# A gated recurrence inside a four-part kernel: a PSUM bank for each gate, the order i, g, o, and the cell in PSUM

## The chip, the cores and the metric

The kernel runs on one core of a Trainium2 chip. The metric is the time on the device in microseconds (us). Three runs of the kernel before gave 1126.01, 1126.28 and 1126.47 us, a median of 1126.28 us.

## The reference

The input `x` has 32 sequences of 256 positions with 128 features; `adj` has a 256x256 matrix for each sequence. Four blocks follow one another, each with a layer normalisation in front and a residual addition behind: a graph convolution on the first 25 positions, a recurrence over all 256 positions, a graph convolution on all of them, and a mixture of eight experts of which two are used for each token. The change touches only the recurrence:

```python
def step(carry, xs):
    h, c = carry
    xi_t, xf_t, xg_t, xo_t = xs
    i_t = jax.nn.sigmoid(xi_t + h @ V_i)
    f_t = jax.nn.sigmoid(xf_t + h @ V_f)
    g_t = jnp.tanh(xg_t + h @ V_c)
    o_t = jax.nn.sigmoid(xo_t + h @ V_o)
    c_new = h * c + i_t * g_t
    h_new = o_t * jnp.tanh(c_new)
    return ((h_new, c_new), h_new)
```

The gate f is computed and never used: the new cell takes `h * c`, not `f * c`. So three gates count, i, g and o. Each of the 256 steps needs the h of the step before it.

## The kernel before

Everything is written out by hand: five instruction queues (TensorE, VectorE, ScalarE, GpSimd, SyncE), each worked off in its order, with semaphores between them. No planner is at work.

The first 90 us or so hold the loads, the preparation of the weights and the small graph convolution. Then come the 256 steps of the recurrence, in 32 groups (`G`) of eight steps (`s` = 0 to 7). Then come the last two blocks, 16 passes over two sequences each.

The state lies transposed: 128 hidden features on the partitions and the 32 sequences along the free dimension. h is kept as two fp16 parts, `h1` (scaled by 1024 and rounded) and `h2` (what is left), and each V matrix as three bf16 parts. One step is this ring:

- TensorE (line 594, the function `gate`) adds `V @ h` onto PSUM, where the input part `U @ x` and the bias already lie. It waits for `h1`, does three products for each of i, o and g, waits for `h2`, and does two products each for i and o, raises `io_ps`, then two for g, and raises `g_ps`. These are 15 matmuls of 32 columns.
- ScalarE takes the sigmoid of i and o together (line 827, 64 elements in each partition, into `S`), then the tanh of g (line 829, into `GC`).
- VectorE forms the new cell with one scan (line 1111). `S` and `GC` interleave two values for each sequence, so that the scan gives first g and then i * g + h * c. The result `CC` lies in SBUF.
- ScalarE takes the tanh of the cell (line 831, `tanh_c`).
- VectorE forms h from o and `tanh_c` twice: as fp16 `h1` (line 1113), which TensorE waits for, and as fp32 `hs` (line 1114). Then come `h2` (line 1116) and the product h * c for the next step (line 1117, into `GC`).

Each engine has other work in its queue behind its part of the step, chosen by `s`. On VectorE this is `fill`: the normalised input of the next group at s = 0 (`xn`, line 1056), the output rows `x2s` at s = 1 (line 1045, which reads PSUM), statistics at s = 2 and 3, at s = 4 a piece of the adjacency matrix and the normalised output `ys` (line 1040), at s = 5 the scaled adjacency matrix `adjs` (line 1090), statistics at s = 6 and 7. On TensorE: transposes of the last group's h at s = 0 (line 611), of `xn` at s = 1 (line 562), the input products `U @ x` of the next group at s = 3, 4 and 5 (`x_gate`, line 568, fp32, 256 columns, two instructions for each), four transposes of `adjs` at s = 6 (line 626), the biases of the next group at s = 7 (line 573). On ScalarE: row sums of the adjacency matrix at s = 0 and 1 (lines 835 and 840), a copy of the transposed input out of PSUM at s = 2 (line 813), and at s = 6 and 7 a small copy (line 844) and a scaled copy of the transposed adjacency matrix into `adjT` (line 845).

The eight PSUM banks in the recurrence: i and o share one bank and g has one, both doubled for alternate groups (banks 0 to 3); bank 4 holds the transposes of `xn`, bank 5 those of h, bank 6 those of `adjs`; bank 7 is free.

Of the kernel before, what the change touches and what calls it, by code (L numbers as in the profile page):

```python
# [21 lines left out]
ALU = mybir.AluOpType  # L22
# [3 lines left out]
P = 128  # L26
# [47 lines left out]
def build(nc, io):  # L74
    x_in, adj_in, out = io["x"], io["adj"], io["out"]

    with ExitStack() as ctx:
# [45 lines left out]
        with ExitStack() as rec:  # L123
# [8 lines left out]
            CC = sb("CC", [P, B, 2], where=rec)  # L132
# [66 lines left out]
        def pair(name, shape, dt=F32):  # L199
# [38 lines left out]
        (io_ps, g_ps, gates_ready, cell_ready, tanh_ready, h1_ready, h32_ready, h2_ready, hc_ready,  # L238
# [3 lines left out]
            "io_ps", "g_ps", "gates_ready", "cell_ready", "tanh_ready", "h1_ready", "h32_ready", "h2_ready", "hc_ready",  # L242
# [21 lines left out]
        g_bank, io_bank = [PB[0], PB[1]], [PB[2], PB[3]]  # L264
        io_v = [p[:].rearrange("p (q n) -> p q n", q=2) for p in io_bank]
# [11 lines left out]
        def iterations(eng, body):  # L277

            body(0, 0, 0)
            with eng.Fori(0, NB2 // 2 - 1) as it:  # L280
                body(it * 2 + 1, 1, it)
                body(it * 2 + 2, 0, it + 1)
            body(NB2 - 1, 1, NB2 // 2 - 1)

# [4 lines left out]
        def _(sp):  # L289
# [53 lines left out]
            sp.wait_ge(adjT_ready, 2 * NGRP)  # L343
# [15 lines left out]
        def _(pool):  # L359
# [23 lines left out]
            tp.memset(S[:], 0.0).then_inc(gates_ready, 1)  # L383
            tp.memset(GC[:], 0.0).then_inc(hc_ready, 1)
# [102 lines left out]
        def _(pe):  # L487
# [77 lines left out]
            def x_gate(k, q):  # L565

                o = g_bank[k][:, 0:STEPS * B] if q == 2 else io_v[k][:, q, :]
                mm(o, us[:, q, :], xbuf[:], start=(q != 1), stop=False, skip_group_check=True)  # L568

            def biases(k):  # L570
                for q in range(3):
                    o = g_bank[k][:, 0:STEPS * B] if q == 2 else io_v[k][:, q, :]
                    mm(o, brow[:, q, :], ones3[:], start=False, stop=False, skip_group_check=True)
# [5 lines left out]
            pe.wait_ge(xbuf_ready, 1)  # L579
            for q in (0, 1, 2):  # L580
                x_gate(0, q)
            biases(0)
            pe.wait_ge(state_ready, 3)

            with pe.Fori(0, NGRP // 4) as it:
                for q4 in range(4):
                    G, k = it * 4 + q4, q4 % 2
                    for s in range(STEPS):
                        t = it * (4 * STEPS) + (q4 * STEPS + s)
                        cols = slice(s * B, (s + 1) * B)  # L590

                        def gate(q, p, h):
                            o = g_bank[k][:, cols] if q == 2 else io_v[k][:, q, cols]
                            return mm(o, vp[p][:, q, :], h[:], start=False, stop=True, skip_group_check=True)  # L594

                        pe.wait_ge(h1_ready, t + 1)
                        for q in (0, 1, 2):
                            for p in range(3):
                                gate(q, p, h1)
                        pe.wait_ge(h2_ready, t + 1)  # L600
                        for q in (0, 1):
                            for p in range(2):
                                m = gate(q, p, h2)
                        m.then_inc(io_ps, 1)
                        for p in range(2):
                            m = gate(2, p, h2)
                        m.then_inc(g_ps, 1)

                        if s == 0:
                            for i in range(2):  # L610
                                m = tr(PB[5][:, i * P:(i + 1) * P], hs[1 - k][:, i * P:(i + 1) * P], ident)
                            m.then_inc(hT_ps, 1)
                        if s == 1:
                            pe.wait_ge(xn_ready, G + 2)
                            x_transpose()
                        if s in (3, 4, 5):
                            if s == 3:
                                pe.wait_ge(xbuf_ready, G + 2)
                            x_gate(1 - k, s - 3)
                        if s == 7:  # L620
                            biases(1 - k)
                        if s == 6:
                            pe.wait_ge(a_scaled, G + 1)
                            for c in range(2):
                                for n in range(2):
                                    m = tr(PB[6][:, c * T + n * P:c * T + (n + 1) * P], adjs[:, n, c * P:(c + 1) * P], ident)  # L626
                            m.then_inc(aT_ps, 1)
            pe.wait_ge(h2_ready, T + 1)
            for i in range(2):
                m = tr(PB[5][:, i * P:(i + 1) * P], hs[1][:, i * P:(i + 1) * P], ident)  # L630
# [77 lines left out]
            pe.wait_ge(adjT_ready, 2 * NGRP)  # L708
# [49 lines left out]
        def _(act):  # L758
# [61 lines left out]
            with act.Fori(0, NGRP // 4) as it:  # L820
                for q4 in range(4):
                    G, k = it * 4 + q4, q4 % 2
                    for s in range(STEPS):
                        t = it * (4 * STEPS) + (q4 * STEPS + s)
                        cols = slice(s * B, (s + 1) * B)
                        act.wait_ge(io_ps, t + 1)
                        av(S[:, :, :, 1], io_v[k][:, :, cols], ACT.Sigmoid, scale=1 / SC)  # L827
                        act.wait_ge(g_ps, t + 1)
                        av(GC[:, :, 0], g_bank[k][:, cols], ACT.Tanh, scale=1 / SC).then_inc(gates_ready, 1)  # L829
                        act.wait_ge(cell_ready, t + 1)  # L830
                        av(tanh_c[:], CC[:, :, 1], ACT.Tanh).then_inc(tanh_ready, 1)  # L831

                        if s == 0:
                            act.wait_ge(adj_loaded[k], it * 32 + (q4 // 2 * 16 + 16))
                            av(junk[:], adjn[k][:, 0, :], ACT.Copy, accum_out=deg[:, 0:1])
                        if s == 2:
                            act.wait_ge(xT_ps, G + 2)
                            x_evacuate().then_inc(xbuf_ready, 1)
                        if s == 1:
                            av(junk[:], adjn[k][:, 1, :], ACT.Copy, accum_out=deg[:, 1:2]).then_inc(deg_ready, 1)  # L840
                        if s in (6, 7):
                            c = s - 6
                            act.wait_ge(aT_ps, G + 1)
                            av(junk[:, 0:1], ident[:, 0:1], ACT.Copy)
                            av(adjT[:, bass.ds(G, 1), c, :].rearrange("p o n -> p (o n)"), PB[6][:, c * T:(c + 1) * T], ACT.Copy,
                               scale=dinv[:, c:c + 1]).then_inc(adjT_ready, 1)
# [64 lines left out]
        def _(dve):  # L911
# [131 lines left out]
            def h_scaled_add(G, i):  # L1043

                return v.scalar_tensor_tensor(out=x2s[:, i, :], in0=PB[5][:, i * P:(i + 1) * P], scalar=1 / SC,
# [57 lines left out]
            with dve.Fori(0, NGRP // 4) as it:  # L1103
                for q4 in range(4):
                    G, k = it * 4 + q4, q4 % 2
                    for s in range(STEPS):
# [4 lines left out]
                        v.tensor_tensor_scan(scan_flat(CC[:]), scan_flat(S[:, 0]), scan_flat(GC[:]), 0.0, ALU.mult, ALU.add).then_inc(cell_ready, 1)  # L1111
# [184 lines left out]
```

## Time and profile before

| | |
|---|---|
| median of three runs | 1126.28 us |
| the profiled execution | 1126.91 us |
| its span, first to last instruction | 1125.1 us |
| mean granted TensorE clock | 0.769 of full speed |
| TensorE matmuls busy | 942.1 us (84%) |
| VectorE busy | 805.4 us (72%) |
| ScalarE busy | 557.3 us (50%) |
| GpSimd busy | 167.4 us (15%) |

The profiled execution's time is its span and 1.8 us around it. The busy shares are averages over the whole kernel; the recurrence has limits of its own, and these are read from the views of that stretch.

### The profile page before, as it was taken

Reading aid. Unit: us, or ns where it says so; the run is one execution under the profiler, and the core shown is the slowest. Engines: PE = TensorE matmul, PEld = TensorE weight load, DVE = VectorE, ACT = ScalarE, POOL = GpSimd, SP = SyncE. Lnnn points to the kernel's source line nnn. Section 1 sums busy time; section 2 is a strip of 40 time slices with the busy share of each in tenths; the row PEclk is TensorE's granted clock in tenths of the full one; section 3 lists DMA queues with packets and bytes.
Section 4 is the critical chain, followed back from the end, with each engine's and each line's share of the span. In section 5 each row is a group of like instructions: output and inputs, shape, how many; then the busy total and the mean of one; then the engine's idle time right before and its main releaser. Section 6 shows DMA issues by size and latency. Waiting matters only on the chain.

```text
span 1125.1 us, 21842 instructions
## 1 busy us (share of the span) xinstructions
PE 942.1 (84%) x6990; PEld 643.4 (57%) x6990; DVE 805.4 (72%) x2993; ACT 557.3 (50%) x1568; POOL 167.4 (15%) x309
## 2 busy tenths in 40 slices
PE   0976777777777777777747999999999999999998
PEld 0754444444444444444425776667677766776765
DVE  4355777777777777777735778877777888777785
ACT  1233444444444444444414666666666666666664
POOL 5501111111111111111111001111010111100000
PEclk9995555555555555555557999999999999999999
DMA  7900111011111111111020000000000000000000
GB/s 203 163 3 20 39 38 37 28 34 36 37 37 33 37 37 37 32 33 33 28 70 19 1 29 29 28 28 28 0 28 28 28 28 28 28 16 12 9 9 19
DMA packets 58323, 39.70 MB, mean 35 GB/s; under 512 B 4191, under 2 KB 57636, under 8 KB 58276
## 3 DMA queue, kind: packets, MB, share of 16 engines
q1 hardware_dynamic: 55971, 36.83, 12.3%
q0 software_dynamic: 656, 2.11, 0.6%
q10 hardware_dynamic: 1674, 0.49, 0.2%
q8 instruction: 11, 0.18, 0.1%
q14 instruction: 11, 0.09, 0.0%
HBM read 26.12 MB, written 13.30 MB: 35 GB/s over the span
## 4 chain that ended last, share of the span: by engine, by line
PE 53%; DVE 27%; ACT 12%; issue 6%; DMA 2%; POOL 0%; SPq 0%; DVEq 0%; POOLq 0%
PE pb L680 13%; PE pb L699 12%; PE pb L594 9%; DVE CC L1111 6%; ACT tanh_c L831 5%; DVE h L1113 4%; ACT S L827 4%; DVE glo L1214 3%; PE pb L626 3%; PE pb L642 3%; PE pb L687 3%; DVE Gw L1210 2%; DVE ys L1040 2%; ACT GC L829 2%; PE pb L653 2%
## 5 line engine op out<-in xcount | busy, mean ns | idle before, releaser
L594 PEld LDWEIGHTS pb<-h,vp 128*128 128x128 bf16 x3840 | 142.2, 106 | 214.0 <-DVE h L1113 211.5
L594 PE MATMUL pb<-h,vp 128*128 128x32 f16 x3840 | 170.3, 191 | 94.0 <-DVE h L1113 86.0
L891 ACT ACTIVATE Gl<-pb,vcols 128x512 f32<-128x512 f32 x256 | 162.3, 685 | 144.8 <-PE pb L680 144.8
L1210 DVE TENSOR_TENSOR Gw<-Gl,pb 128x1024 f32<-128x1024 f32 x128 | 155.8, 1217 | 103.1 <-PE pb L687 92.6
L1214 DVE TENSOR_TENSOR glo<-Gw,ghi 128x1024 fp32r<-128x1024 f32 x128 | 157.7, 1232 | 0.0
L827 ACT ACTIVATE S<-pb 128x64 f32<-128x64 f32 x256 | 58.2, 227 | 162.4 <-PE pb L594 162.4
L871 ACT ACTIVATE ghi<-Gw 128x1024 fp32r<-128x1024 f32 x128 | 135.1, 1055 | 1.7 <-DVE Gw L1210 1.7
L568 PE MATMUL pb<-xbuf,us 128*128 128x256 f32 x198 | 118.2, 703 | 0.6 <-ACT xbuf L813 0.6
L680 PE MATMUL pb<-xhi,w1hi 128*128 128x512 f32 x256 | 115.6, 452 | 0.0
L1111 DVE TENSOR_TENSOR_SCAN CC<-S,GC 128x64 f32<-128x64 f32 x256 | 74.4, 291 | 51.7 <-ACT GC L829 46.2
L831 ACT ACTIVATE tanh_c<-CC 128x32 f32<-128x32 f32 x256 | 59.0, 231 | 93.5 <-DVE CC L1111 93.5
L699 PE MATMUL pb<-ghi,w2hi 128*128 128x512 f32 x256 | 103.1, 403 | 0.9 <-DVE glo L1214 0.9
L1113 DVE SCALAR_TENSOR_TENSOR h<-S,tanh_c 128x32 f16<-128x32 f32 x256 | 49.3, 192 | 75.9 <-ACT tanh_c L831 75.9
L699 PE MATMUL pb<-glo,w2hi 128*128 128x512 f32 x256 | 101.8, 397 | 0.0
L699 PE MATMUL pb<-ghi,w2lo 128*128 128x512 f32 x256 | 101.6, 397 | 0.0
L680 PE MATMUL pb<-xhi,w1lo 128*128 128x512 f32 x256 | 101.5, 396 | 0.0
L680 PE MATMUL pb<-xlo,w1hi 128*128 128x512 f32 x256 | 100.4, 392 | 0.0
L680 PEld LDWEIGHTS pb<-xhi,w1hi 128*128 128x128 f32 x256 | 48.6, 190 | 21.5 <-issue 15.0
L699 PEld LDWEIGHTS pb<-ghi,w2hi 128*128 128x128 f32 x256 | 48.1, 188 | 19.0 <-issue 7.0
L1116 DVE TENSOR_TENSOR h<-hs,h 128x32 f16<-128x32 f32 x256 | 49.2, 192 | 8.9
L680 PEld LDWEIGHTS pb<-xlo,w1hi 128*128 128x128 f32 x256 | 48.5, 189 | 11.4
L699 PEld LDWEIGHTS pb<-glo,w2hi 128*128 128x128 f32 x256 | 48.2, 188 | 11.7
(223 smaller groups left out, 1470.1 us busy)
## 6 DMA issues: line engine op xcount, KB each, us to landing
adjn<-in_adj SPq DMA_DIRECT2D x32, 256.0 KB, 2.7
x_d<-x2s SPq DMA_DIRECT2D x33, 128.0 KB, 1.8
y_d<-ys SPq DMA_DIRECT2D x33, 128.0 KB, 1.8
yr<-y_d SPq DMA_DIRECT2D x16, 256.0 KB, 2.8
x2r<-x_d SPq DMA_DIRECT2D x16, 256.0 KB, 3.1
out<-outb SPq DMA_DIRECT2D x16, 256.0 KB, 2.3
X<-in_x SPq DMA_DIRECT2D x4, 912.0 KB, 17.5
aW<-in_L_gnn_W SPq DMA_DIRECT2D x2, 640.0 KB, 10.8
```

The costliest lines, as they stand in the source:

```text
L568: mm(o, us[:, q, :], xbuf[:], start=(q != 1), stop=False, skip_group_check=True)
L594: return mm(o, vp[p][:, q, :], h[:], start=False, stop=True, skip_group_check=True)
L680: m = mm(H[e % 2][c][:], w[:, e, c * P:(c + 1) * P], x[par][:], start=(k == 0), stop=(k == 2))
L699: m = mm(yT_b[:], w[:, e, c, :], g[e % 4][:, c, :], start=False, stop=(e == E - 1 and k == 6), skip_group_check=True)
L827: av(S[:, :, :, 1], io_v[k][:, :, cols], ACT.Sigmoid, scale=1 / SC)
L831: av(tanh_c[:], CC[:, :, 1], ACT.Tanh).then_inc(tanh_ready, 1)
L871: av(ghi[e % 4][:], Gw[e % 2][:], ACT.Copy).then_inc(ghi_ready, 1)
L891: a = av(Gl[e % 2][:, c, :], PB[2 * (e % 2) + c][:], ACT.Gelu, bias=eb1[:, e, c:c + 1])
L1111: v.tensor_tensor_scan(scan_flat(CC[:]), scan_flat(S[:, 0]), scan_flat(GC[:]), 0.0, ALU.mult, ALU.add).then_inc(cell_ready, 1)
L1113: v.scalar_tensor_tensor(out=h1[:], in0=S[:, 1, :, 1], scalar=SC, in1=tanh_c[:], op0=ALU.mult, op1=ALU.mult).then_inc(h1_ready, 1)
L1210: v.tensor_tensor(Gw[e % 2][:], Gl[e % 2][:], bc(PB[5][:].unsqueeze(1), [P, 2, 4 * P]), ALU.mult).then_inc(gw_ready, 1)
L1214: v.tensor_tensor(glo[e % 4][:], Gw[e % 2][:], ghi[e % 4][:].bitcast(F32), ALU.subtract).then_inc(glo_ready, 1)
```

## The change

Each gate gets a PSUM bank of its own, doubled for alternate groups: i in banks 2 and 3, o in 6 and 7, g in 0 and 1. The order on TensorE is i, g, o in both halves of the products, and each gate has a semaphore of its own. ScalarE takes the sigmoid of i (32 elements in each partition), the tanh of g, and then the sigmoid of o as an instruction of its own. `gates_ready`, for which the scan waits, is still raised by the tanh of g; o raises `o_ready`, for which VectorE waits in front of its wait for the tanh of the cell. `CC` becomes a part of PSUM bank 5. All transposes share bank 4, and so TensorE waits at s = 0 for the last copy of `adjT`, and at s = 2 for the `x2s` of the group. The side work moves: the transposes of `xn` from s = 1 to s = 2, the copy of them on ScalarE from s = 2 to s = 3, the biases from s = 7 to s = 3 (they now start the bank), the three `x_gate` from s = 3, 4, 5 to s = 4, 5, 7. One small memset on GpSimd gives `adjT_ready` a count of one at the start. Below, in the first part left out, the semaphore `io_ps` is replaced by `i_ps`, and `o_ps` and `o_ready` are added.

```diff
--- before.py
+++ after.py
@@ -129,7 +129,7 @@
...
-            CC = sb("CC", [P, B, 2], where=rec)
+            CCseed = sb("CCseed", [P, 1], where=rec)
...
@@ -235,11 +235,11 @@
...
@@ -261,8 +261,7 @@
...
-        g_bank, io_bank = [PB[0], PB[1]], [PB[2], PB[3]]
-        io_v = [p[:].rearrange("p (q n) -> p q n", q=2) for p in io_bank]
+        gate_bank = [[PB[2], PB[6], PB[0]], [PB[3], PB[7], PB[1]]]
...
@@ -281,6 +280,8 @@
...
+
+        CC = PB[5][:, 0:2 * B].rearrange("p (b k) -> p b k", k=2)
...
@@ -340,7 +341,7 @@
...
-            sp.wait_ge(adjT_ready, 2 * NGRP)
+            sp.wait_ge(adjT_ready, 2 * NGRP + 1)
...
@@ -381,6 +382,7 @@
...
+            tp.memset(CCseed[:], 0.0).then_inc(adjT_ready, 1)
...
@@ -562,24 +564,21 @@
                     m = tr(PB[4][:, i * P:(i + 1) * P], xn[:, i, :], ident)
                 m.then_inc(xT_ps, 1)
 
-            def x_gate(k, q):
-
-                o = g_bank[k][:, 0:STEPS * B] if q == 2 else io_v[k][:, q, :]
-                mm(o, us[:, q, :], xbuf[:], start=(q != 1), stop=False, skip_group_check=True)
-
             def biases(k):
                 for q in range(3):
-                    o = g_bank[k][:, 0:STEPS * B] if q == 2 else io_v[k][:, q, :]
-                    mm(o, brow[:, q, :], ones3[:], start=False, stop=False, skip_group_check=True)
+                    mm(gate_bank[k][q][:, 0:STEPS * B], brow[:, q, :], ones3[:], start=True, stop=False, skip_group_check=True)
+
+            def x_gate(k, q):
+                mm(gate_bank[k][q][:, 0:STEPS * B], us[:, q, :], xbuf[:], start=False, stop=False, skip_group_check=True)
 
             pe.wait_ge(x1_ready, 2)
             pe.wait_ge(xn_ready, 1)
             x_transpose()
             pe.wait_ge(setup_ready, 1)
             pe.wait_ge(xbuf_ready, 1)
+            biases(0)
             for q in (0, 1, 2):
                 x_gate(0, q)
-            biases(0)
             pe.wait_ge(state_ready, 3)
 
             with pe.Fori(0, NGRP // 4) as it:
@@ -590,44 +589,43 @@
                         cols = slice(s * B, (s + 1) * B)
 
                         def gate(q, p, h):
-                            o = g_bank[k][:, cols] if q == 2 else io_v[k][:, q, cols]
-                            return mm(o, vp[p][:, q, :], h[:], start=False, stop=True, skip_group_check=True)
+                            return mm(gate_bank[k][q][:, cols], vp[p][:, q, :], h[:], start=False, stop=True, skip_group_check=True)
 
                         pe.wait_ge(h1_ready, t + 1)
-                        for q in (0, 1, 2):
+                        for q in (0, 2, 1):
                             for p in range(3):
                                 gate(q, p, h1)
                         pe.wait_ge(h2_ready, t + 1)
-                        for q in (0, 1):
+                        for q, done in ((0, i_ps), (2, g_ps), (1, o_ps)):
                             for p in range(2):
                                 m = gate(q, p, h2)
-                        m.then_inc(io_ps, 1)
-                        for p in range(2):
-                            m = gate(2, p, h2)
-                        m.then_inc(g_ps, 1)
+                            m.then_inc(done, 1)
 
                         if s == 0:
+                            pe.wait_ge(adjT_ready, G * 2 + 1)
                             for i in range(2):
-                                m = tr(PB[5][:, i * P:(i + 1) * P], hs[1 - k][:, i * P:(i + 1) * P], ident)
+                                m = tr(PB[4][:, i * P:(i + 1) * P], hs[1 - k][:, i * P:(i + 1) * P], ident)
                             m.then_inc(hT_ps, 1)
-                        if s == 1:
+                        if s == 2:
                             pe.wait_ge(xn_ready, G + 2)
+                            pe.wait_ge(x2_ready, G + 1)
                             x_transpose()
-                        if s in (3, 4, 5):
-                            if s == 3:
+                        if s == 3:
+                            biases(1 - k)
+                        if s in (4, 5, 7):
+                            if s == 4:
                                 pe.wait_ge(xbuf_ready, G + 2)
-                            x_gate(1 - k, s - 3)
-                        if s == 7:
-                            biases(1 - k)
+                            x_gate(1 - k, (4, 5, 7).index(s))
                         if s == 6:
                             pe.wait_ge(a_scaled, G + 1)
                             for c in range(2):
                                 for n in range(2):
-                                    m = tr(PB[6][:, c * T + n * P:c * T + (n + 1) * P], adjs[:, n, c * P:(c + 1) * P], ident)
+                                    m = tr(PB[4][:, c * T + n * P:c * T + (n + 1) * P], adjs[:, n, c * P:(c + 1) * P], ident)
                             m.then_inc(aT_ps, 1)
             pe.wait_ge(h2_ready, T + 1)
+            pe.wait_ge(adjT_ready, 2 * NGRP + 1)
             for i in range(2):
-                m = tr(PB[5][:, i * P:(i + 1) * P], hs[1][:, i * P:(i + 1) * P], ident)
+                m = tr(PB[4][:, i * P:(i + 1) * P], hs[1][:, i * P:(i + 1) * P], ident)
             m.then_inc(hT_ps, 1)
 
 
@@ -705,7 +703,7 @@
...
-            pe.wait_ge(adjT_ready, 2 * NGRP)
+            pe.wait_ge(adjT_ready, 2 * NGRP + 1)
...
@@ -823,17 +821,19 @@
                     for s in range(STEPS):
                         t = it * (4 * STEPS) + (q4 * STEPS + s)
                         cols = slice(s * B, (s + 1) * B)
-                        act.wait_ge(io_ps, t + 1)
-                        av(S[:, :, :, 1], io_v[k][:, :, cols], ACT.Sigmoid, scale=1 / SC)
+                        act.wait_ge(i_ps, t + 1)
+                        av(S[:, 0, :, 1], gate_bank[k][0][:, cols], ACT.Sigmoid, scale=1 / SC)
                         act.wait_ge(g_ps, t + 1)
-                        av(GC[:, :, 0], g_bank[k][:, cols], ACT.Tanh, scale=1 / SC).then_inc(gates_ready, 1)
+                        av(GC[:, :, 0], gate_bank[k][2][:, cols], ACT.Tanh, scale=1 / SC).then_inc(gates_ready, 1)
+                        act.wait_ge(o_ps, t + 1)
+                        av(S[:, 1, :, 1], gate_bank[k][1][:, cols], ACT.Sigmoid, scale=1 / SC).then_inc(o_ready, 1)
                         act.wait_ge(cell_ready, t + 1)
                         av(tanh_c[:], CC[:, :, 1], ACT.Tanh).then_inc(tanh_ready, 1)
 
                         if s == 0:
                             act.wait_ge(adj_loaded[k], it * 32 + (q4 // 2 * 16 + 16))
                             av(junk[:], adjn[k][:, 0, :], ACT.Copy, accum_out=deg[:, 0:1])
-                        if s == 2:
+                        if s == 3:
                             act.wait_ge(xT_ps, G + 2)
                             x_evacuate().then_inc(xbuf_ready, 1)
                         if s == 1:
@@ -842,7 +842,7 @@
...
-                            av(adjT[:, bass.ds(G, 1), c, :].rearrange("p o n -> p (o n)"), PB[6][:, c * T:(c + 1) * T], ACT.Copy,
+                            av(adjT[:, bass.ds(G, 1), c, :].rearrange("p o n -> p (o n)"), PB[4][:, c * T:(c + 1) * T], ACT.Copy,
...
@@ -1042,7 +1042,7 @@
...
-                return v.scalar_tensor_tensor(out=x2s[:, i, :], in0=PB[5][:, i * P:(i + 1) * P], scalar=1 / SC,
+                return v.scalar_tensor_tensor(out=x2s[:, i, :], in0=PB[4][:, i * P:(i + 1) * P], scalar=1 / SC,
...
@@ -1108,7 +1108,8 @@
                         cols = slice(s * B, (s + 1) * B)
                         dve.wait_ge(hc_ready, t + 1)
                         dve.wait_ge(gates_ready, t + 2)
-                        v.tensor_tensor_scan(scan_flat(CC[:]), scan_flat(S[:, 0]), scan_flat(GC[:]), 0.0, ALU.mult, ALU.add).then_inc(cell_ready, 1)
+                        v.tensor_tensor_scan(scan_flat(CC), scan_flat(S[:, 0]), scan_flat(GC[:]), 0.0, ALU.mult, ALU.add).then_inc(cell_ready, 1)
+                        dve.wait_ge(o_ready, t + 1)
                         dve.wait_ge(tanh_ready, t + 1)
                         v.scalar_tensor_tensor(out=h1[:], in0=S[:, 1, :, 1], scalar=SC, in1=tanh_c[:], op0=ALU.mult, op1=ALU.mult).then_inc(h1_ready, 1)
                         v.scalar_tensor_tensor(out=hs[k][:, cols], in0=S[:, 1, :, 1], scalar=SC, in1=tanh_c[:], op0=ALU.mult, op1=ALU.mult).then_inc(h32_ready, 1)
```

## Rows read from the trace of the kernel before

**Rows 1.** The page: shares of the chain that ended last, by line
```profile
PE pb L680 13%; PE pb L699 12%; PE pb L594 9%; DVE CC L1111 6%; ACT tanh_c L831 5%; DVE h L1113 4%; ACT S L827 4%; DVE glo L1214 3%; PE pb L626 3%; PE pb L642 3%; PE pb L687 3%; DVE Gw L1210 2%; DVE ys L1040 2%; ACT GC L829 2%; PE pb L653 2%
```

**Rows 2.** Windows: length, busy of PE, PEld, DVE, ACT, POOL, granted clock, DMA share, GB/s
```profile
300.00:400.00 100.00, 75.72 (x924) 48.22 (x923) 71.81 (x405) 42.86 (x225) 18.51 (x42) 0.50 0.11 34
640.00:1125.00 485.00, 478.62 (x2152) 335.50 (x2150) 384.64 (x857) 308.12 (x443) 42.65 (x42) 1.00 0.07 22
```

**Rows 3.** The chain, h1 of s = 0 to h1 of s = 1: start, length, what
```profile
421.33 0.20 DVE h L1113
...
421.58 0.63 PE pb L594 x13
422.24 0.23 ACT S L827
422.46 0.10 ACT GC L829
...
422.58 0.30 DVE CC L1111
422.91 0.24 ACT tanh_c L831
...
423.17 0.20 DVE h L1113
```

**Rows 4.** Timelines of that step: start, length, instruction, count
```profile
421.58 0.42 PE L594 MATMUL pb<-h,vp 128*128 128x32 f16 x9 [0.66 <-DVE h L1113]
421.66 0.19 DVE L1116 TENSOR_TENSOR h<-hs,h 128x32 f16<-128x32 f32 x1
...
421.91 0.34 PE L594 MATMUL pb<-h,vp 128*128 128x32 f16 x6
...
422.36 0.19 ACT L829 ACTIVATE GC<-pb 128x32 f32<-128x32 f32 x1
...
423.05 0.40 ACT L840 ACTIVATE junk<-adjn 128x256 f32<-128x256 f32 x1
```

**Rows 5.** Groups by line and shape, 120 to 594 us: count, busy, mean ns, idle before
```profile
L831 ACT ACTIVATE tanh_c<-CC 128x32 f32<-128x32 f32 x242 | 55.8, 231 | 88.4 <-DVE CC L1111 88.4
L827 ACT ACTIVATE S<-pb 128x64 f32<-128x64 f32 x242 | 55.0, 227 | 151.3 <-PE pb L594 151.3
L829 ACT ACTIVATE GC<-pb 128x32 f32<-128x32 f32 x242 | 47.0, 194 | 0.0
...
L1076 DVE SCALAR_TENSOR_TENSOR adjn<-const,sdiag,adjn 128x128 f32<-128x128 f32 x60 | 20.7, 345 | 0.1
...
L1045 DVE SCALAR_TENSOR_TENSOR x2s<-pb,X 128x128 f32<-128x128 f32 x62 | 15.2, 286 | 0.5 <-PE pb L630 0.5
```

**Rows 6.** Timeline, VectorE at the end of s = 4 and in s = 5
```profile
429.48 0.60 DVE L1040 TENSOR_SCALAR ys<-x2s,mv_y,rs_y 128x128 f32<-128x128 f32 x2
...
429.99 0.28 DVE L1111 TENSOR_TENSOR_SCAN CC<-S,GC 128x64 f32<-128x64 f32 x1
```

**Rows 7.** Timeline, the transposes of s = 6 and what follows them
```profile
431.77 1.12 PE L626 MATMUL pb<-const,adjs 128*128 128x128 f32 x4 [0.29 <-DVE adjs L1090]
...
433.04 0.46 ACT L845 ACTIVATE adjT<-pb,dinv 128x256 f32 x1
...
433.40 0.22 ACT L827 ACTIVATE S<-pb 128x64 f32<-128x64 f32 x1
433.50 0.20 ACT L829 ACTIVATE GC<-pb 128x32 f32<-128x32 f32 x1
```

**Rows 8.** Timeline, TensorE in s = 4 and the start of s = 5
```profile
427.09 0.67 PE L594 MATMUL pb<-h,vp 128*128 128x32 f16 x15
...
427.60 1.20 PE L568 MATMUL pb<-xbuf,us 128*128 128x256 f32 x2
...
428.92 0.67 PE L594 MATMUL pb<-h,vp 128*128 128x32 f16 x15
```

**Rows 9.** Timeline, the sigmoid of s = 1 of the next group
```profile
437.07 0.23 ACT L827 ACTIVATE S<-pb 128x64 f32<-128x64 f32 x1 [0.54 <-PE pb L594]
```

More of the change, by code:

```diff
@@ L236, in build @@
             "state_ready", "var_a", "rstd_a", "dgs_ready", "dgr_ready", "rstd_first", "var_first", "tiny_ready", "whi_ready"))
-        (io_ps, g_ps, gates_ready, cell_ready, tanh_ready, h1_ready, h32_ready, h2_ready, hc_ready,
+        (i_ps, g_ps, o_ps, o_ready, gates_ready, cell_ready, tanh_ready, h1_ready, h32_ready, h2_ready, hc_ready,
          xn_ready, xT_ps, xbuf_ready, hT_ps, x2_ready, x2_stored, y_stats, y_aggr, y_rstd, y_ready, y_stored,
@@ L241, in build @@
             sem(n) for n in (
-            "io_ps", "g_ps", "gates_ready", "cell_ready", "tanh_ready", "h1_ready", "h32_ready", "h2_ready", "hc_ready",
+            "i_ps", "g_ps", "o_ps", "o_ready", "gates_ready", "cell_ready", "tanh_ready", "h1_ready", "h32_ready", "h2_ready", "hc_ready",
             "xn_ready", "xT_ps", "xbuf_ready", "hT_ps", "x2_ready", "x2_stored", "y_stats", "y_aggr", "y_rstd",
```

## The prediction

> **What bounds the kernel now.** I read the page's chain first: which lines carry the end [rows 1]. The two heaviest (680 and 699, TensorE's) belong to the last block; the lines of the recurrence are 594, 1111, 831, 1113, 827 and 829. The windows separate the two [rows 2]. In the recurrence no engine is full (in 100 us TensorE 75.7, VectorE 71.8, ScalarE 42.9), and the granted TensorE clock is 0.50, the lower of its two levels (1.2 GHz); from 640 us on TensorE is busy for 478.6 of 485 us at 1.00. The edit leaves that last part alone. So the question is the latency of one ring through three engines, 256 times.
>
> The chain in order of time shows the ring [rows 3]: h1 at 421.33, matmuls at 421.58, sigmoid at 422.24, tanh of g behind it, scan at 422.58, tanh of the cell at 422.91, next h1 at 423.17. That is 1.84 us: 0.25 from h1 to the matmuls, 0.66 to the sigmoid, 0.34 to the scan, 0.33 to the tanh, 0.26 to h1. A group, from the sigmoid at 422.24 to the same one eight steps later at 437.07, takes 14.83 us [rows 3, 9], and eight plain steps would take 14.72. 32 groups are 474.6 us.
>
> The matmuls one by one [rows 4]: nine with h1 start at 421.58; each record is 0.19 long and the nine end after 0.42, so they start every 0.03 us. h2 ends at 421.85. The six with h2 start at 421.91 and end 0.34 later, again every 0.03. So the 13th starts at 421.97 to 422.00 (I use 422.00, the last being at 422.06), and the sigmoid of i and o, which waits for it, starts 0.24 later. The tanh of g starts at 422.36. Its own last matmul (422.06 + 0.24 = 422.30) would allow 422.30: it stands behind the sigmoid of 64 elements, which takes the queue for 0.12.
>
> **Order i, g, o and own sigmoid for i.** In the new order i is complete with the 11th matmul (421.94) and g with the 13th. Sigmoid of i: 421.94 + 0.24 = 422.18. The tanh of g may start when its products are there, 422.24, and when the queue is free: 64 elements take 227 ns and 32 take 194 [rows 5], so the 32 saved are worth 0.033, and the queue is taken for 0.12 - 0.03 = 0.09, to 422.27. Later of the two: 422.27 instead of 422.36, a gain of 0.09 us. Bounds: 0.12 if the products alone decide; 0.04 if each wait costs the queue 0.14. The sigmoid of o (about 194 ns) follows at about 422.36 and ends at 422.56, before the tanh of the cell is due at about 422.8: it lies beside the scan. Without that cover it would cost its place in the queue, 0.09. The new wait for o has h1, hs, h2, line 1117 and the fill behind it on VectorE, and TensorE waits for h1; but o is there 0.5 us before the tanh's end, so the wait is passed while VectorE idles. Cost nothing; the scan too starts 0.03 after its releaser although two waits stand in front of it.
>
> Splitting the banks costs no instruction: 15 matmuls as before, six of `x_gate`, three biases.
>
> **Where the 0.09 doesn't arrive.** Three steps of eight are not held by ScalarE's tanh of g.
> - s = 5: the two `ys` instructions start at 429.48 and the scan stands behind them, at 429.99 [rows 6]. That is fixed by the h1 of s = 4: the gates of s = 5 start at 428.92 [rows 8], so that h1 started 0.25 before, at 428.67, and its scan comes 1.32 behind it, against 1.25 in a plain step. Gain in this step: none.
> - s = 6 and 7: the transposes of `adjs` start at 431.77, which hangs on VectorE's work behind the h1 of s = 5. They end at 432.89; ScalarE stands in its queue waiting for them, copies at 433.04, and only at 433.40 takes the sigmoid of s = 7, with g at 433.50 [rows 7]. All of it is fixed by h1 of s = 5. So what s = 6 wins is lost in this wait, and s = 7 wins 0.01, the shorter first sigmoid.
> So 5 x 0.09 + 0.01 = 0.46 us in each group.
>
> **Cell in PSUM.** The tanh now reads PSUM. ScalarE with 32 elements takes 231 ns from SBUF and 194 from PSUM [rows 5]: 0.037 gained, on the chain. The scan now writes PSUM, and no row shows VectorE doing that. The nearest are its reads: a scalar_tensor_tensor of 128 elements takes 345 ns from SBUF alone and 286 with one operand in PSUM [rows 5], so placement moves an instruction of VectorE by 0.059. I bound the write by that size on either side, -0.06 to +0.06, and take +0.03: the write is on the ring with its acknowledgement, unlike a read. Net gain c = 0.037 - 0.03 = 0.007, from -0.02 to +0.10. It counts in the seven steps with h1 on the chain (s = 0 to 5 and 7; s = 6 vanishes in the wait of above): 0.05 us. Line 1117 reads the cell from PSUM; by the same rows such a read isn't dearer. If it were, by 0.06, the chains through `ys` and `adjs` would lengthen by it, 0.12 a group.
> The Trainium skill, Perfetto Trace Analysis, section Optimizing Scalar/DVE Operations, gives about 60 ns of access overhead for VectorE on SBUF and 125 on PSUM, and 93 for ScalarE on SBUF and 51 on PSUM. The trace agrees on ScalarE (0.037 of its 0.042) and doesn't on VectorE's reads. By the page, as an estimate, the cell's move would lose 0.023 in a step; that would turn the forecast's sum into that of rival B.
>
> **Side work.** `x_gate` at s = 4 starts 0.51 behind the gates and ends 1.71 behind them; the next gates come at 1.83 [rows 8]. The new step is 1.84 - 0.09 - 0.007 = 1.74, so 0.03 is left. The gain in this step is capped at 0.12. s = 3 now has the biases in place of `x_gate`, and s = 7 has `x_gate`: its gates start no later than 433.40 - 0.66 = 432.74, so it ends by 434.45; the next gates are due at 433.49 + 0.22 + 0.33 + 0.26 + 0.25 = 434.55. The transposes of `xn` at s = 2 wait for `x2s`, two instructions of 0.29 behind line 1117 [rows 5], ready some 0.9 behind the gates; four transposes take 1.12 [rows 7], two some 0.7: done at 1.6 of 1.74. The transposes of h at s = 0 wait for the copy to `adjT`, 0.46 long and 0.2 behind the tanh of the cell, so done at 0.7 from there; their turn comes behind the gates, at 0.26 + 0.25 + 0.5 = 1.0, 0.3 to spare. The copy of the input at s = 3 lies behind the tanh, where it lay at s = 2. All hidden; the memset lies in the setup, which has long ended on GpSimd. SyncE's and GpSimd's queues keep order; their inputs are late by nothing.
>
> **Sum.** 0.46 + 0.05 = 0.51 us a group, x 32 = 16.3 us. The profiled execution took 1126.91 us, 0.63 above the median; less 16.3 this is 1110.6, and from the median 1110.0. I say 1110.5 us.
>
> **Rivals.**
> - A, the write to PSUM is free (or gains). For: VectorE's reads show no price. Against: nothing shows a write. c = 0.037: 0.46 + 7 x 0.037 = 0.72 a group, 23 us, 1104 us. With the outer bound (c = 0.097) 36 us, 1090; the cap at s = 4 and those behind `ys` make that unlikely.
> - B, the write costs the whole 0.06, more than the tanh saves: c = -0.023, 0.46 - 0.16 = 0.30 a group, 9.6 us, 1117 us. For: the size of the placement effect in the rows. Against: its sign there.
> - C, ScalarE's queue takes 0.14 for each instruction that waits (as from the tanh of the cell at 422.91 to the row sum behind it at 423.05 [rows 3, 4]). Then g gains 0.04, and s = 7 loses 0.04: 0.20 - 0.04 + 0.05 = 0.21 a group, 6.7 us, 1120 us.
> - D, slower. Place: the scan to the tanh of the cell, seven times a group. The change turns slower when the write costs more than 0.037 + 0.46/7 = 0.10 us; at 0.15 it loses 7 x 0.113 - 0.46 = 0.33 a group, 10.6 us, 1137 us. For: the acknowledgement of a VectorE write to PSUM is nowhere in the trace. Against: no placement difference in the rows is over 0.06.
> - E, no gain: one of the moved pieces holds the ring. If `x_gate` really occupies TensorE some 0.1 longer than its modelled end, the steps s = 4, 5 and 7 fall back to the old length; that takes 0.09 of the sum, and nothing more since s = 5 is held by `ys`. To reach zero the wait at s = 0 or s = 2 would have to bind as well, against the 0.3 that each has.
>
> **How the numbers follow.** Forecast 0.50, A 0.22, B 0.13, C 0.06, D 0.05, E 0.04. A measurement of this kernel can tell about 0.2%, 2.3 us, from no change. Faster: forecast, A, B and nearly all of C: 0.89. D gives slower 0.06 with some of E; the rest, 0.05, is the same. Range: forecast 1106 to 1114, by a write between +0.01 and +0.05; A reaches to 1101, B and C to 1120. I give 1100 to 1120.
>
> **What would show it.** In the profile after: a plain step of 1.74 us; tanh of g starting about 0.09 after the sigmoid of i; 0.22 from there to the scan, as before; the tanh of the cell at about 194 ns; the scan's duration tells the price of the write directly (0.28 to 0.30 before [rows 3, 6], 0.32 if I am right). The idle of h1 must still end by `tanh_c`, not by the sigmoid of o. In s = 5 the scan still follows `ys`, and in s = 7 the sigmoid still follows the copy to `adjT`, whatever the rest. A group of 14.3 us. Wrong would be: a scan of 0.39 or more, matmuls of the gates that start behind `x_gate` instead of h1, or a granted clock other than 0.50 in the recurrence.

## The result, and the profile after

| | before | after |
|---|---|---|
| median | 1126.32 us (4 runs, 1126.01 to 1126.47) | 1138.59 us (4 runs, 1137.54 to 1140.12) |
| the profiled execution | 1126.91 us | 1137.54 us |
| its span | 1125.1 us | 1135.7 us |

The ratio is 1.0108, with a 95% interval of 1.0092 to 1.0124: the kernel became 12.3 us slower. The forecast was 1110.5 us, with a range of 1100 to 1120.

The plain step did become shorter, but not by what was forecast. This is the chain after, from the h1 of s = 3 to the h1 of s = 4 (start, length, what), which answers to [rows 3]:

```profile
434.36 0.20 DVE h L1114
...
434.60 0.58 PE pb L592 x11
...
435.21 0.20 ACT S L825
435.41 0.10 ACT GC L827
...
435.53 0.31 DVE pb L1111
...
435.86 0.20 ACT tanh_c L831
...
436.09 0.02 DVEq L1113
...
436.16 0.19 DVE h L1114
```

From h1 to h1 it is 1.80 us, against 1.84. From the matmuls to the scan it is 0.93, where [rows 3] had 1.00: the new order of the gates brings what it should. From the scan to the tanh it is 0.33 as before. But from the tanh of the cell to h1 it is 0.30, where [rows 3] had 0.26, although the tanh itself has become shorter. The tanh ends at 436.06 and h1 starts 0.10 later; before, the distance was 0.02. Between the two now stands a piece of VectorE's instruction queue (DVEq), line 1113: the wait for the tanh, as an instruction of its own.

The groups by line and shape after, 120 to 594 us (count, busy, mean ns, idle before), answer to [rows 5]:

```profile
L1111 DVE TENSOR_TENSOR_SCAN pb<-S,GC 128x64 f32<-128x64 f32 x241 | 72.4, 301 | 47.2 <-ACT GC L827 18.7 <-issue 18.7
L829 ACT ACTIVATE S<-pb 128x32 f32<-128x32 f32 x241 | 50.2, 208 | 0.0
L825 ACT ACTIVATE S<-pb 128x32 f32<-128x32 f32 x240 | 47.6, 198 | 153.4 <-PE pb L592 153.4
L831 ACT ACTIVATE tanh_c<-pb 128x32 f32<-128x32 f32 x241 | 47.5, 197 | 87.5 <-DVE pb L1111 87.5
L827 ACT ACTIVATE GC<-pb 128x32 f32<-128x32 f32 x241 | 46.9, 194 | 0.0
```

The tanh of the cell takes 197 ns instead of 231. The scan takes 301 with its output in PSUM, against 291 to SBUF: the write costs 0.010 us. And the scan has 18.7 us of idle in front of it that is put down to "issue", that is, to no releaser at all; in the kernel before the scan has none of this. VectorE's waits in the recurrence (in total, times, longest) show how it is spread:

```profile
DVE h L1114 <- ACT tanh_c L831: 85.0, 256, 0.3
...
DVE pb L1111 <- issue: 18.7, 7, 2.9
DVE x2s L1045 <- issue: 1.6, 8, 0.2
```

Seven idle times of up to 2.9 us. Each is at the end of a pass of VectorE's loop: 32 groups in a loop over four have seven such ends. (The eight of 0.2 us in `x2s`, one in each pass, are small; what they wait for the trace doesn't say.) The timeline around the first of them:

```profile
151.15 0.19 ACT L827 ACTIVATE GC<-pb 128x32 f32<-128x32 f32 x1
151.23 0.21 ACT L829 ACTIVATE S<-pb 128x32 f32<-128x32 f32 x1
151.35 0.69 POOL L457 TENSOR_TENSOR rs_x<-ve_x,mhalf 128x2 f32<-128x2 f32 x1
153.68 0.30 DVE L1111 TENSOR_TENSOR_SCAN pb<-S,GC 128x64 f32<-128x64 f32 x1 [2.68 <-issue]
154.01 0.20 ACT L831 ACTIVATE tanh_c<-pb 128x32 f32<-128x32 f32 x1 [2.57 <-DVE pb L1111]
```

The tanh of g is done at 151.34, so the scan could start at 151.37. It starts at 153.68. In the queues, one transfer falls into 151.3 to 153.7 (packets, MB, share of 16 engines):

```profile
q14 instruction: 1, 0.01, 1.3%
```

Over the whole execution that queue has, first before and then after:

```profile
q14 instruction: 11, 0.09, 0.0%
```
```profile
q14 instruction: 47, 0.39, 0.1%
```

36 loads of instructions more, 0.30 MB, so some 8 KB each and five for each of the seven loop ends. In the built program, VectorE's loop holds 315 instructions before and 347 after. The 32 more are the waits for o, one for each step of four groups.

The distances from scan to scan in one group, read from the timeline, put this together (the fifth is the step behind `ys`, the seventh the one behind the transposes of `adjs`):

```
before                     1.84 1.84 1.84 1.83 1.90 1.83 1.91 1.84   14.83
after                      1.80 1.80 1.79 1.81 1.93 1.80 1.97 1.80   14.70
after, last group of pass  1.82 1.80 1.81 1.81 1.94 1.79 1.97 4.10   17.04
```

The row "after" is one group; the groups without a loop end take from 14.68 to 14.82. From the first scan to the last it is 472.8 us before and 485.9 after. The seven loop ends take 28.6 us where seven plain steps would take 12.6: 16.0 us lost. The shorter groups give 2.9 of it back. Where ScalarE and VectorE hold the ring in s = 5, 6 and 7 it went as forecast: the scan stands behind `ys`, and the sigmoid of s = 7 behind the copy to `adjT`; these lines of the timeline after answer to [rows 6, 7]:

```profile
422.17 0.60 DVE L1040 TENSOR_SCALAR ys<-x2s,mv_y,rs_y 128x128 f32<-128x128 f32 x2
...
422.68 0.29 DVE L1111 TENSOR_TENSOR_SCAN pb<-S,GC 128x64 f32<-128x64 f32 x1
...
424.51 1.11 PE L623 MATMUL pb<-const,adjs 128*128 128x128 f32 x4 [0.28 <-DVE adjs L1090]
...
425.77 0.46 ACT L845 ACTIVATE adjT<-pb,dinv 128x256 f32 x1
...
426.13 0.19 ACT L825 ACTIVATE S<-pb 128x32 f32<-128x32 f32 x1
426.21 0.20 ACT L827 ACTIVATE GC<-pb 128x32 f32<-128x32 f32 x1
```

The granted clock in the recurrence is 0.50 as in [rows 2].

### The profile page after: what moved, and what is told of

Its sections match the earlier page's. It is cut to its first block, busy times and chain, and to the rows that moved or that the text cites. A ratio compares the mean times of both kernels' runs of the same rounds, so it can differ in the third digit from the quotient of the medians.

```text
span 1135.7 us, 22412 instructions
## 1 busy us (share of the span) xinstructions
PE 939.4 (83%) x6990; PEld 643.1 (57%) x6990; DVE 806.2 (71%) x2993; ACT 565.3 (50%) x1824; POOL 166.8 (15%) x310
## 3 DMA queue, kind: packets, MB, share of 16 engines
q1 hardware_dynamic: 55971, 36.83, 12.3%
## 4 chain that ended last, share of the span: by engine, by line
PE 50%; DVE 29%; ACT 9%; issue 9%; DMA 2%; DVEq 1%; POOL 0%; SPq 0%; POOLq 0%
PE pb L678 13%; PE pb L697 12%; PE pb L592 6%; DVE pb L1111 6%; ACT tanh_c L831 4%; DVE h L1114 4%; PE pb L623 3%; DVE glo L1215 3%; PE pb L640 3%; PE pb L685 3%; ACT S L825 2%; DVE Gw L1211 2%; DVE ys L1040 2%; PE pb L651 2%; DVE xh L1163 1%
## 5 line engine op out<-in xcount | busy, mean ns | idle before, releaser
L825 ACT ACTIVATE S<-pb 128x32 f32<-128x32 f32 x256 | 50.7, 198 | 165.3 <-PE pb L592 165.3
L1111 DVE TENSOR_TENSOR_SCAN pb<-S,GC 128x64 f32<-128x64 f32 x256 | 76.9, 300 | 53.5 <-ACT GC L827 24.3
L831 ACT ACTIVATE tanh_c<-pb 128x32 f32<-128x32 f32 x256 | 50.4, 197 | 92.0 <-DVE pb L1111 92.0
```

What stands on the lines that cost most here:

```text
L825: av(S[:, 0, :, 1], gate_bank[k][0][:, cols], ACT.Sigmoid, scale=1 / SC)
L1111: v.tensor_tensor_scan(scan_flat(CC), scan_flat(S[:, 0]), scan_flat(GC[:]), 0.0, ALU.mult, ALU.add).then_inc(cell_ready, 1)
```

## The experiments

Two theories were put side by side at first. Theory W: the wait for o costs twice, once because its 32 instructions make VectorE's loop too long to stay loaded, and once because of where it puts the wait for the tanh. The rival: the cell in PSUM is what costs. The ratio of each run is against the kernel before on the same chip, whose median was 1125.55 us for the first four runs, 1126.25 for the next four and 1126.38 for the last two. Where two runs are subtracted that were on different chips, these medians say what the chips can add: up to 0.8 us.

**Without the wait for o** (`e1_no_o_wait`). ScalarE works in order and takes the sigmoid of o ahead of the tanh of the cell, so that the wait for the tanh covers both.

```diff
-                        dve.wait_ge(o_ready, t + 1)
                         dve.wait_ge(tanh_ready, t + 1)
```

> The changed kernel without VectorE's wait for o (ScalarE works in order, so the tanh of the cell implies it). Theory W: the 32 added wait instructions in VectorE's loop (347 instead of 315) cause an instruction load at each of the 7 loop ends (2.3 us each, 16 us), and since the builder puts the wait for tanh into the instruction of its own, h1 starts 0.07 us later in seven steps of each group (0.07 x 7 x 32 = 15.7 us). Both go: 1138.6 - 16 - 16 = about 1107 us, h1 0.03 behind the tanh, no 2 us gap in VectorE. Rival P (the cell in PSUM is what costs): no change, 1138. Rival L (the stall comes from the grown loop of ScalarE or TensorE): the gaps stay, 1123.

Measured: 1107.16 us, ratio 0.9834 (0.9818 to 0.9851). The chain of one step (start, length, what), and below it VectorE's waits, in which the loop ends no longer appear:

```profile
424.53 0.20 DVE h L1113
...
424.78 0.58 PE pb L592 x11
...
425.38 0.20 ACT S L825
425.58 0.10 ACT GC L827
...
425.70 0.31 DVE pb L1111
...
426.04 0.21 ACT tanh_c L831
...
426.27 0.20 DVE h L1113
```
```profile
DVE h L1113 <- ACT tanh_c L831: 67.5, 256, 0.3
...
DVE st_x L1094 <- issue: 0.2, 1, 0.2
DVE adjn L1076 <- issue: 0.2, 1, 0.2
```

A step of 1.74, with 0.23 from the tanh to h1. The rival that the cell in PSUM costs, and the one that the grown loops of ScalarE or TensorE cause the gaps, are out: the cell and these two loops are as in the changed kernel, and the gaps are gone.

**The kernel before with one satisfied wait more** (`e2_before_more_waits`).

```diff
                         dve.wait_ge(tanh_ready, t + 1)
+                        dve.wait_ge(hc_ready, t + 1)
```

> The kernel before, with one wait more in front of each h1, for a semaphore that has long been reached; the wait for the tanh stays on h1 itself. VectorE's loop has 347 instructions, nothing else changes. Theory W: 7 gaps of 2.3 us at the loop ends and no late h1: 1126.3 + 16 = 1142. Rivals P and L: 1126, as before.

Measured: 1141.94 us, ratio 1.0143 (1.0126 to 1.0160). The group keeps its 14.83 us, and the loop ends get their gaps:

```profile
DVE CC L1111 <- issue: 18.9, 7, 2.9
```

A wait that never waits costs 16 us here, by its room in the loop alone.

**The two waits in the other order** (`e3_o_wait_behind`).

```diff
-                        dve.wait_ge(o_ready, t + 1)
                         dve.wait_ge(tanh_ready, t + 1)
+                        dve.wait_ge(o_ready, t + 1)
```

> The changed kernel with the two waits in front of h1 in the other order of source lines. The instruction of its own then carries o, and h1 carries the tanh. Theory W: h1 starts 0.03 behind the tanh, not 0.10, worth 15.7 us; the 7 gaps stay: 1138.6 - 15.7 = 1123. Rival P: no change, 1138.

Measured: 1124.36 us, ratio 0.9989 (0.9979 to 0.9999). The listing of the built program shows h1 with one wait and the second as an instruction of its own in front of it; of these two, the wait written last is the one that stands alone. In the changed kernel that was the tanh, the late one; here it is o. The timeline (start, length, instruction):

```profile
422.35 0.20 ACT L831 ACTIVATE tanh_c<-pb 128x32 f32<-128x32 f32 x1 [0.28 <-DVE pb L1111]
...
422.57 0.19 DVE L1114 SCALAR_TENSOR_TENSOR h<-S,tanh_c 128x32 f16<-128x32 f32 x1 [0.26 <-ACT tanh_c L831]
```

h1 starts 0.02 behind the tanh's end, and not 0.10. The gaps are still there; step and group are those of `e1_no_o_wait`. So, by these runs, the late wait standing alone costs 1138.6 - 1124.4 = 14.2 us, and the loads 1124.4 - 1107.2 = 17.2 us.

**The cell in SBUF** (`e4_cell_sbuf`).

```diff
-        CC = PB[5][:, 0:2 * B].rearrange("p (b k) -> p b k", k=2)
+            CC = sb("CC", [P, B, 2], where=rec)
```

> The changed kernel with the cell in SBUF, everything else kept. Theory W: the tanh of the cell takes 231 instead of 197 ns, the scan 291 instead of 301; 0.024 to 0.034 a step in seven steps of a group, 5 to 8 us slower: 1144 to 1146, gaps and late h1 unchanged. Rival P: faster than 1138, at the forecast's 0.10 a step by 23 us, 1116.

Measured: 1146.44 us, ratio 1.0186 (1.0169 to 1.0203). 7.8 us slower than the changed kernel: the move of the cell is a gain.

**VectorE's loop over two groups** (`e5_dve_loop_halved`). From here on the question was what "too long" means.

```diff
-            with dve.Fori(0, NGRP // 4) as it:
-                for q4 in range(4):
+            with dve.Fori(0, NGRP // 2) as it:
+                for q4 in range(2):
```

> The changed kernel with VectorE's loop alone written over two groups instead of four: 175 instructions in its body and 16 passes; the late h1 stays. Theory W (a body of 347 instructions is too long to stay loaded): no 2 us gap at all, 1138.6 - 16.4 = 1122. Rival N (each taken loop end costs a load once waits stand in the body, whatever its length): 15 gaps instead of 7, 1138.6 + 8 x 2.3 = 1157.

Measured: 1122.69 us, ratio 0.9972 (0.9960 to 0.9985). No gap, though there are 15 loop ends instead of 7, and the wait for o and the late h1 are still there. A loop end by itself costs nothing here. That leaves the late wait alone: 1122.7 - 1107.2 = 15.5 us.

**A body of 331** (`e6_loop_331`), on the kernel without the wait for o.

```diff
                         dve.wait_ge(tanh_ready, t + 1)
+                        if q4 < 2:
+                            dve.wait_ge(hc_ready, t + 1)
```

> The kernel without the wait for o (315 instructions, 1107.2 us, no gap), with 16 waits more in VectorE's loop, all long satisfied, in front of h1 in the first two groups of each pass: 331 instructions. Theory W leaves open from where between 315 and 347 a pass has to be loaded: 1107 if the bound lies above 331, 1107 + 16 = 1123 if below. A cost that grows with the number of waits instead (rival N2): half of it, 1115.

Measured: 1124.06 us, ratio 0.9980 (0.9970 to 0.9989). VectorE's waits:

```profile
DVE pb L1111 <- issue: 19.0, 7, 2.9
```

Half the instructions, the whole price (1124.1 - 1107.2 = 16.9 us): it is a threshold, and for a body that begins where this one does it lies between 315 and 331.

**A body of 347 that begins 64 instructions later** (`e7_loop_347_shifted`).

```diff
+            for n in range(128):
+                dve.wait_ge((x1_ready, tiny_ready)[n % 2], 2)
             with dve.Fori(0, NGRP // 4) as it:
```

These waits are for constants, and in the built program two of them go into one instruction: 128 waits are 64 instructions.

> The changed kernel with 64 instructions more on VectorE, satisfied waits, ahead of its loop; the body keeps 347 but begins at another place of the instruction stream. Where only the body's length decides (theory W), the 7 gaps stay: 1138.6 plus up to 2 us for the added instructions, about 1140. Where the place of the body against the blocks in which instructions are loaded decides (rival B), the gaps may go: 1122 to 1124.

Measured: 1151.60 us, ratio 1.0233 (1.0215 to 1.0251), worse than either theory said. VectorE's timeline at the first loop end:

```profile
155.86 0.30 DVE L1114 TENSOR_TENSOR_SCAN pb<-S,GC 128x64 f32<-128x64 f32 x1 [2.65 <-issue]
158.05 0.19 DVE L1117 SCALAR_TENSOR_TENSOR h<-S,tanh_c 128x32 f16<-128x32 f32 x1 [1.89 <-issue]
```

Each pass now has a second stall, between its third instruction (the scan) and its fifth (h1). In the trace's instruction queue the first load of this pass starts at 153.87 us and the second at 156.27, behind the scan of 155.86. So the start of the body and what follows the scan come in two loads, and a border between two blocks of instructions lies between them. Place matters, and the place of one border is now known.

**The kernel without the wait for o, cell in SBUF** (`e8_no_o_wait_cell_sbuf`): the two edits of `e1_no_o_wait` and `e4_cell_sbuf` together.

> The kernel without the wait for o, and with the cell in SBUF: the gate order, the banks and the moved side work alone. Theory W: scan 291 and tanh 231 ns, 0.024 us a step in seven steps of a group, 1107.2 + 5.4 = 1112.6, up to 1115 as the move of the cell measured 7.8 us in the changed kernel. Rival P (a cell in PSUM costs time): below 1107.

Measured: 1113.53 us, ratio 0.9891 (0.9874 to 0.9907). The step is 1.76 us. Gate order, banks and moved side work alone are worth 12.7 us (1126.25 - 1113.53), the cell in PSUM 6.4.

**The kernel before, its loop begun 32 instructions later** (`e9_before_shifted_32`), with the edit of `e7_loop_347_shifted` and 64 waits instead of 128.

> The kernel before with 32 satisfied waits more on VectorE ahead of its loop; the loop itself is untouched, 315 instructions. Theory B (instructions are loaded in blocks, of some 128 by the 8 KB of a load, and a body that lies in one block more than the buffer keeps is loaded in each pass): bodies of 331 and 347 had gaps and 315 had none, so 315 ends just short of a block; moved by 32 it reaches into the next and gets 7 gaps: 1126.3 + 16 = 1142, or more with a second stall a pass, as the shift by 64 gave. Rival W (the length of the body alone decides): 1126 to 1128, no gap.

Measured: 1141.51 us, ratio 1.0131 (1.0114 to 1.0148). VectorE's waits, in a kernel whose loop is the old one, word for word:

```profile
DVE CC L1114 <- issue: 18.4, 7, 2.7
```

**The changed kernel, its loop begun 90 instructions later** (`e10_shifted_90`), with 180 waits.

> The changed kernel with 90 satisfied waits more on VectorE ahead of its loop, the body untouched at 347. Theory B: from the two bounds the body began 54 to 63 instructions into a block; 90 further it begins 16 to 25 into the next, and 347 end inside three blocks: no gap, 1138.6 - 16 = 1122, plus up to 3 us for the added instructions. Rival W: 1138.6 plus 3, 7 gaps.

Measured: 1128.53 us, ratio 1.0023 (1.0013 to 1.0033). VectorE's waits:

```profile
DVE h L1117 <- ACT tanh_c L831: 85.1, 256, 0.3
...
DVE pb L1114 <- issue: 9.5, 1, 9.5
```

No gap at a loop end, with 347 instructions and the wait for o. The 9.5 us are ahead of the first scan, where the changed kernel idles 4.9; the rest is there with the 90 added instructions. The first scan comes at 98.3 us instead of 92.5, and that is why 1122 was not reached. From first to last scan it is 469.3 us, as in `e5_dve_loop_halved` (469.4). Length alone is refuted by these two, and the place of the body against the block borders is confirmed from both sides.

## Why the prediction was wrong

Point by point, in the order in which the prediction took them:

- **Order i, g, o, own sigmoid for i: right.** Forecast 0.09 a step and 14.7 us in all. From the matmuls to the scan it is 0.92 to 0.93 instead of 1.00, and `e8_no_o_wait_cell_sbuf` has a step of 1.76 against 1.84, thus 0.08, and 12.7 us in all. The sigmoid of i holds ScalarE's queue for 0.09 to 0.10, as worked out.
- **"Cost nothing" for the wait for o: wrong, and here the prediction failed, twice.** It said that the wait is passed while VectorE idles, since o is there early. That is true of o and beside the point. First, the wait that stands alone was not that for o, but that for the tanh, the last to come, and h1 was passed on only behind it: some 0.07 us in each h1, 14 to 16 us. The evidence brought for it, that two waits stand in front of the scan, was read too shallowly: there the early one (`hc_ready`) is carried by a register instruction ahead and the late one by the scan itself, which is the arrangement that `e3_o_wait_behind` gives h1. Second, an instruction that costs no time on its engine still takes room. 32 more in the loop body cost some 17 us, and no step of the prediction counted them. It counted what each queue waits for, and not how long each loop is.
- **Where the gain doesn't arrive (s = 5, 6, 7): right.** In `e1_no_o_wait` the scans are 1.72 to 1.75 apart, but 1.87 behind `ys` and 1.96 behind the transposes of `adjs`, 14.23 a group (forecast 14.3).
- **Cell in PSUM: right in sign, too small.** Taken: a write of +0.03 and a gain of 0.007 a step. Measured: the scan 0.010 longer, the tanh 0.034 shorter, 0.02 to 0.03 in the step, 6.4 to 7.8 us in all, where the forecast had 1.6. The size 0.03 for the write had no row behind it but a bound from the reads, and those showed no price. The Trainium skill, Perfetto Trace Analysis, section Optimizing Scalar/DVE Operations, is borne out for ScalarE (its 0.042 is 0.034 here) and not for a VectorE write (its 0.065 is 0.010).
- **Side work: right.** No matmul of the gates stood behind `x_gate`. The tightest place was the forecast's: at s = 4 of `e1_no_o_wait`, `x_gate` ends 0.03 before the next gates start, and they start 0.25 behind h1 as in any step.
- **Rivals.** D gave 1137 us, within 2 us of the result, by another mechanism: it asked for a write of 0.15 us, and the write measured 0.010. The time came out near by chance. The slower side had been given 0.06. For the cell alone A came nearest (0.037 a step, against 0.024 from the two durations). C is out: the sigmoid holds ScalarE's queue for 0.10 and not 0.14. No rival named the place of a wait or the length of a loop.

The sum with what was measured: 1126.3, less 18.7 for the change without its wait (ratio 0.9834), plus 14.2 for the late wait standing alone, plus 17.2 for the loads, is 1139.0, against 1138.6. It has to close, because both prices are differences of the same three runs. Added singly to `e1_no_o_wait` they measured 15.5 (`e5_dve_loop_halved`) and 16.9 (`e6_loop_331`), which gives 1140.0. So each is known to 1 or 2 us. Without the two prices the forecast's 16.3 would have been somewhat low: 2.0 too much for the gates, and 4.8 too little for the cell.

What keeps a body loaded can be read from the times at which the instruction loads start. These are five in a row from one pass of three kernels (us):

```
changed kernel             213.2  215.6  226.7  248.6  270.4
e7, begins 64 later        216.6  219.0  221.5  242.6  264.6
e9, begins 32 later        214.7  217.1  223.1  247.0  271.0
```

The first is at the loop end, the second once the body runs again. Set against the scans and the listing, the last three of the changed kernel start when VectorE is at about the 71st, 201st and 326th instruction of its body; in `e9_before_shifted_32` it is about the 39th, 163rd and 291st, and in `e7_loop_347_shifted` the last two are at about the 136th and 262nd. So there is one load of 8 KB for each 128 instructions, and the borders move with the start of the body. With blocks of 128 every run fits one rule: a body inside three blocks stays loaded, one that touches a fourth doesn't, and the old start lies 54 to 63 into a block. The stall of `e7_loop_347_shifted` between the body's third and fifth instruction puts it 67 or 68 before a border, thus 60 or 61 into a block, and that is where the loads are too. A body that touches four blocks has five loads in a pass, so one block more than it needs is being loaded at its end; that this is what pushes the first one out is worked out from the count and not shown by itself. Why the second load of a pass doesn't start before the first has let the body run on stays open.

The Trainium skill, Runtime: NRT & Kernel Launch, section Instruction fetch mechanics, says that most engines keep 512 instructions, loaded in blocks of 256, and that a taken branch whose target is outside the two blocks has to wait for a load. In kind that is what the runs show, on a body of 347, far below 512. The size of the block isn't: by the page, a body that begins 182 to 197 instructions into a block fits with 315 and doesn't with 331, which agrees with the gaps. That is an estimate from its figures. But its loads would be 256 instructions apart, and VectorE's are some 128 apart.

The fastest version is `e1_no_o_wait`, the change without its wait for o: 1107.16 us, 1.66% below the kernel before, and faster than the changed kernel by 31 us.

## What to carry to other kernels

Count the instructions of each engine's loop body, waits included, before and after an edit. An instruction whose wait is long satisfied can push a body over the border up to which it stays loaded, and instructions ahead of the loop can do the same or undo it; the sign in the profile is idle time put down to issue, once in each pass, with a load in an instruction queue beside it. Where an instruction has two waits, the last to come should be the one that it carries itself; and where one engine's order already implies a wait, leave it out.

## What the runs showed of the hardware that was not expected

- A wait instruction that is satisfied at once costs the step nothing while it stands ahead of a later wait (14.83 us a group with and without it, `e2_before_more_waits`). One that is the last to be satisfied puts the instruction behind it off by some 0.07 us (h1 starts 0.10 behind the tanh's end in the changed kernel, 0.02 in `e3_o_wait_behind`).
- A loop end on VectorE whose target is no longer loaded costs 2.2 to 2.5 us (16.0 us in seven); one whose target is loaded costs nothing that the scan distances show (1.80 us at a loop end in `e5_dve_loop_halved`, as within).
- VectorE's instructions come in loads of 8 KB, one for each 128 instructions of the body (loads at about the 71st, 201st and 326th instruction). A body of 347 stayed loaded or not by its start alone (`e10_shifted_90` against the changed kernel).
- The kernel before was itself near that border: 32 instructions ahead of its loop, none inside, made it 15 us slower.
- A VectorE scan of 64 elements takes 301 ns into PSUM and 291 into SBUF; a tanh of 32 elements takes 197 ns from PSUM and 231 from SBUF.
